# A decoder layer on one core: the steps of a round in another order on all engines

## What is computed

```python
x = _layernorm(x + _L0_attn_ref(x, ...))        # causal self attention, 16 heads of 16
#   local: softmax over the tokens before this one; latent: 4 heads over 50 averages of token pairs
#   gate = sigmoid(local @ gl_w + remote_h @ gr_w); mixed = gate*local + (1-gate)*remote_h; mixed @ out_w
x = _layernorm(x + _L0_xattn_ref(x, ctx, ctx))  # cross attention; queries and keys are normed in each head
x = _layernorm(x + _L0_ffn_ref(x, ...))         # top-1 of 8 experts, 200 tokens each; the rest pass through
```

## Time and profile before

| | us |
|---|---|
| median of 3 runs | 1654.99 |
| lowest and highest of them | 1653.84, 1660.99 |
| the profiled execution | 1657.47 |
| its span, first to last instruction | 1655.7 |

### The profile page before, as it was taken

How to read it: one execution, slowest core, us unless ns; L and a number is a source line. 1 busy time by engine, 2 the same in 40 slices (tenths; PEclk the granted TensorE clock), 3 DMA queues, 4 the chain that set the end, 5 groups by cost and what they waited for, 6 DMA issues and landing times.

```text
span 1655.7 us, 34010 instructions
## 1 busy us (share of the span) xinstructions
PE 1302.4 (79%) x11098; PEld 956.2 (58%) x11098; DVE 830.3 (50%) x2482; ACT 676.3 (41%) x1611; POOL 346.3 (21%) x485
## 2 busy tenths in 40 slices
PE   2577888788888878888888888887888888875886
PEld 2345666566565555555655566565555556554775
DVE  4255455555555555555555555555555555533332
ACT  0234444444444444444444444444444444533111
POOL 2122222221122222222222221122222222110111
PEclk8678777877777787888878787778777887755998
DMA  5233333323332232233333233332233233115452
GB/s 167 49 77 78 78 80 80 76 69 69 79 79 67 70 74 75 68 70 79 79 79 79 69 72 68 79 79 68 69 74 75 67 71 76 45 35 178 161 180 73
DMA packets 187013, 134.99 MB, mean 82 GB/s; under 512 B 95799, under 2 KB 182763, under 8 KB 186735
## 3 DMA queue, kind: packets, MB, share of 16 engines
q1 hardware_dynamic: 181778, 127.50, 30.7%
q0 software_dynamic: 3200, 6.61, 1.3%
q10 hardware_dynamic: 1984, 0.23, 0.1%
HBM read 91.06 MB, written 43.00 MB: 81 GB/s over the span
## 4 chain that ended last, share of the span: by engine, by line
PE 60%; issue 13%; DVE 9%; ACT 6%; POOL 6%; DMA 2%; ACTq 1%; SPq 1%; DVEq 0%; POOLq 0%
PE MI L809 12%; PE MI L810 11%; PE MI L1006 4%; PE MX L1122 3%; PE MX L975 3%; PE ST L993 3%; PE ST L870 3%; DVE negmax_x L1428 3%; DVE negmax_s L1421 3%; PE ST L875 3%; PE MX L837 2%; PE MI L955 2%; PE MX L843 2%; POOL mixed L711 2%; PE MI L919 2%
## 5 line engine op out<-in xcount | busy, mean ns | idle before, releaser
L1428 DVE TENSOR_REDUCE negmax_x<-MX 100x1 bf16<-100x361 f32 x512 | 258.0, 531 | 187.2 <-PE MX L975 185.1
L975 PE MATMUL MX<-stacked,Qst 96*128 96x361 f16 x512 | 180.5, 386 | 101.1 <-DVE negmax_x L1428 65.0
L1191 ACT ACTIVATE wide<-ST 128x800 f32<-128x800 f32 (+1 forms) x256 | 166.5, 665 | 144.9 <-PE ST L993 144.9
L975 PEld LDWEIGHTS MX<-stacked,Qst 96*128 96x128 f16 x512 | 52.6, 109 | 174.5 <-DVE negmax_x L1428 101.1
L993 PE MATMUL ST<-Qst,stacked 112*128 112x200 f16 x768 | 132.4, 301 | 0.2 <-ACT wide L1191 0.2
L700 POOL TENSOR_TENSOR QKhl<-QK,QKhl 128x900 f16<-128x900 f32 x32 | 60.5, 1892 | 182.8 <-ACT QKhl L1198 182.8
L993 PEld LDWEIGHTS ST<-Qst,stacked 112*128 112x128 f16 x768 | 82.2, 122 | 26.6 <-issue 11.2
L837 PE MATMUL MX<-mask_q,identb 100*128 100x400 bf16 (+1 forms) x128 | 43.0, 424 | 65.1 <-DVE negmax_s L1421 27.9
L1485 DVE TENSOR_TENSOR qn<-qc,rsq 128x200 f32<-128x200 f32 x32 | 11.8, 367 | 163.3 <-ACT rsq L1250 163.3
L1006 PE MATMUL MI<-wide,Vx 128*32 128x100 f32 (+1 forms) x3072 | 78.5, 261 | 1.3 <-ACT wide L1191 1.3
L734 POOL COPY x2w<-extra 100x2 f32 (+1 forms) x32 | 8.0, 248 | 340.8 <-issue 328.5
(11 more groups left out here) (259 smaller groups left out, 3050.5 us busy)
## 6 DMA issues: line engine op xcount, KB each, us to landing
stacked<-key_halves SPq DMA_DIRECT2D x96, 180.5 KB, 4.4
self_halves<-QKhl SPq DMA_DIRECT2D x32, 450.0 KB, 3.0
cT<-in_cT SPq DMA_DIRECT2D x32, 361.0 KB, 3.8
key_halves<-Khl SPq DMA_DIRECT2D x32, 361.0 KB
self_stack<-self_halves SPq DMA_DIRECT2D x64, 150.0 KB, 3.9
Qst<-query_halves SPq DMA_DIRECT2D x96, 100.0 KB, 2.6
early<-in_w SPq DMA_DIRECT2D x8, 1024.0 KB
self_stack<-self_halves SPq DMA_DIRECT2D x32, 225.0 KB, 3.8
```

The lines of the kernel that those rows point to most:

```text
L975: pe.matmul(MX[:, n % 2, 0:M], Qst[p][0:96, n * S:n * S + 128], Kst[p][0:96, n // 2 * M:(n // 2 + 1) * M], start=True, stop=True).then_inc ...
L1191: act.activation(cross_part(Px, u), ST[0:n, first:first + 2, 0:width], ACT.Exp).then_inc(st_exp, 1)
L1428: dve.tensor_reduce(negmax_x[:, n:n + 1], MX[0:S, n % 2, 0:M], X, ALU.max, negate=True).then_inc(max_read, 1)
```

## The change

The same steps run on each engine with the same waits, in another order. Besides the order within `body`, the list `MISC` is another one, so some steps take the other MI bank and wait for another step's copy. `MAXIMA` holds the same sequence, only broken into lines at another place.

```diff
--- before.py
+++ after.py
@@ -57,11 +57,11 @@
 OFFSET = {"T": -2, "Y": -1, "X": 0, "K": 1, "A": 2, "B": 1}
 
 
-MISC = ["A1", "A2", "K1", "B1", "T2", "K2", "B2", "T3", "K3", "T4", "B3", "K4", "B4", "T5", "A4",
-        "B5", "T6", "X1", "B6", "B7", "Y1", "K5", "Y2", "A6", "K6", "A7"]
-
...
+MISC = ["A1", "A2", "K1", "T2", "B1", "K2", "K3", "B2", "T3", "T4", "B3", "K4", "T5", "B4", "A4", "T6", "B5",
+        "B6", "X1", "B7", "Y1", "K5", "A6", "K6", "A7", "Y2"]
+
...
 
 SCORES = ["Y0", "Y1", "Y2", "Y3", "Y4", "Y5", "Y6", "Y7", "As0", "As1", "As2"]
 
@@ -600,17 +600,18 @@
             load_x(Seq(0))
 
             def body(it):
+                if it.n + 2 < B:
+                    load_n(Seq(it.n + 2, it.j))
                 if it.n + 3 < B:
                     load_x(Seq(it.n + 3, it.j))
-                if it.n + 2 < B:
-                    load_c(Seq(it.n + 2, it.j))
-                    load_n(Seq(it.n + 2, it.j))
                 if it.has("A"):
                     stack_self(it)
                 if it.has("K"):
                     stack_keys(it)
                 if it.has("B"):
                     stack_queries(it)
+                if it.n + 2 < B:
+                    load_c(Seq(it.n + 2, it.j))
 
             iterations(sp, body)
 
@@ -745,11 +746,10 @@
                 if a: pair_sums(A)
                 if b: gate_local(Bs, it)
                 if a: self_lo(it)
-                if b: gate_remote(Bs, it)
-                if b: mix(Bs)
+                if b: gate_remote(Bs, it); mix(Bs); query_low(it)
                 if t: keep_x2(T)
+                if b: x1_bias(Bs)
                 if t: scatter(T)
-                if b: query_low(it); x1_bias(Bs)
 
             iterations(pool, body)
 
@@ -1044,54 +1044,54 @@
 
             def body(it):
                 a, k, b, x, y, t = (it.has(stage) for stage in "AKBXYT")
+                if x: cross_maximum(it, 0)
                 if a: A1(it); A2(it)
                 if y: cross_scores(it, 0)
                 if k: K12(it, 0)
-                if x: cross_maximum(it, 0); cross_maximum(it, 1)
-                if b: B1(it)
+                if x: cross_maximum(it, 1)
                 if t: T2(it)
                 if x: cross_maximum(it, 2)
+                if b: B1(it)
                 if k: K12(it, 1)
-                if y: cross_scores(it, 1); cross_scores(it, 2)
+                if y: cross_scores(it, 1)
                 if x: cross_maximum(it, 3); cross_maximum(it, 4)
+                if k: K34(it, 0)
+                if x: cross_maximum(it, 5)
                 if b: B2(it)
-                if x: cross_maximum(it, 5)
                 if t: T3(it)
                 if x: cross_maximum(it, 6)
-                if y: cross_scores(it, 3)
-                if k: K34(it, 0)
+                if y: cross_scores(it, 2); cross_scores(it, 3)
                 if x: cross_maximum(it, 7); cross_maximum(it, 8)
                 if t: T4(it)
                 if x: cross_maximum(it, 9)
+                if y: cross_scores(it, 4)
                 if b: B3(it)
-                if y: cross_scores(it, 4)
                 if x: cross_maximum(it, 10)
                 if k: K34(it, 1)
-                if x: cross_maximum(it, 11)
+                if x: cross_maximum(it, 11); cross_maximum(it, 12)
+                if t: T5(it)
+                if y: cross_scores(it, 5)
+                if a: self_maxima(it, 0)
                 if b: B4(it)
-                if x: cross_maximum(it, 12)
-                if a: self_maxima(it, 0)
-                if y: cross_scores(it, 5)
-                if t: T5(it)
                 if a: self_maxima(it, 1)
-                if x: cross_maximum(it, 13); cross_maximum(it, 14)
+                if y: cross_scores(it, 6)
+                if x: cross_maximum(it, 13)
                 if a: A4(it)
-                if y: cross_scores(it, 6)
+                if t: T6(it)
                 if b: B5(it)
-                if x: cross_maximum(it, 15)
-                if t: T6(it)
+                if x: cross_maximum(it, 14); cross_maximum(it, 15)
+                if b: B6(it)
                 if y: cross_scores(it, 7)
                 if x: X1(it)
-                if b: B6(it)
-                if a: self_scores(it, 0); self_scores(it, 1)
+                if a: self_scores(it, 0)
                 if b: B7(it)
-                if a: self_scores(it, 2)
+                if a: self_scores(it, 1); self_scores(it, 2)
                 if y: Y1(it)
                 if k: K56(it, [0, 1])
-                if y: Y2(it)
                 if a: A6(it)
                 if k: K56(it, [2])
                 if a: A7(it)
+                if y: Y2(it)
 
             iterations(pe, body)
 
@@ -1275,35 +1275,35 @@
                 a, k, b, x, y, t = (it.has(stage) for stage in "AKBXYT")
                 if y: cross_exp(it, 0)
                 if k: K12(it, 0)
+                if t: copy_out("T2", it, OxT[:], halves)
                 if b: copy_out("B1", it, latT[:], lambda ps: ps[0:64, 0:S])
-                if t: copy_out("T2", it, OxT[:], halves)
                 if a: self_hi(it)
                 if k: K12(it, 1)
-                if y: cross_exp(it, 1); cross_exp(it, 2)
-                if t: rstd(it.of("T"), rs2, ln2, mv2, t_ln, t_rs)
+                if y: cross_exp(it, 1)
                 if k: K34(it, 0)
+                if y: cross_exp(it, 2)
                 if b: gate_exp(it)
-                if t: copy_out("T4", it, x2T[:], halves)
                 if y: cross_exp(it, 3)
+                if t: rstd(it.of("T"), rs2, ln2, mv2, t_ln, t_rs); copy_out("T4", it, x2T[:], halves)
+                if k: high_k(it, 0)
                 if b: copy_out("B3", it, mixT[:], halves)
-                if k: high_k(it, 0)
                 if y: cross_exp(it, 4)
                 if k: K34(it, 1)
+                if y: cross_exp(it, 5); cross_exp(it, 6)
                 if b: rstd(it.of("B"), rs1, ln1, mv1, b_ln, b_rs)
-                if y: cross_exp(it, 5)
+                if a: A4(it)
+                if b: copy_out("B5", it, x1T[:], halves)
+                if k: high_k(it, 1)
                 if t: router_exp(it)
-                if a: A4(it)
-                if k: high_k(it, 1)
-                if y: cross_exp(it, 6)
-                if b: copy_out("B5", it, x1T[:], halves)
+                if b: B6(it)
                 if y: cross_exp(it, 7)
                 if x: X1(it)
-                if b: B6(it)
-                if a: self_exp(it, 0); self_exp(it, 1)
+                if a: self_exp(it, 0)
                 if b: B7(it)
-                if a: self_exp(it, 2)
+                if a: self_exp(it, 1)
                 if b: high_q(it)
                 if y: copy_out("Y1", it, OxU[:], lambda ps: ps[:, 0:4 * S], (filled["Y2"], it.of("Y").done(back=1)))
+                if a: self_exp(it, 2)
                 if k: values(it, [0, 1])
                 if a: copy_out("A6", it, OsT[:], lambda ps: ps[:, 0:5 * S], (filled["A7"], it.of("A").done(back=1)))
                 if k: values(it, [2])
@@ -1575,32 +1575,31 @@
 
             def body(it):
                 a, k, b, x, y, t = (it.has(stage) for stage in "AKBXYT")
+                if x: cross_max(it, 0)
                 if a: A1(it); A2(it)
-                if x: cross_max(it, 0); cross_max(it, 1)
-                if x: cross_max(it, 2); cross_max(it, 3); cross_max(it, 4); cross_max(it, 5)
+                if x: cross_max(it, 1); cross_max(it, 2); cross_max(it, 3); cross_max(it, 4); cross_max(it, 5)
                 if b: B2(it)
                 if t: T3(it)
-                if b: gate_sum(it)
+                if b: gate_sum(it); gating(it)
                 if t: norm2(it)
-                if x: cross_max(it, 6); cross_max(it, 7)
-                if b: gating(it)
+                if x: cross_max(it, 6); cross_max(it, 7); cross_max(it, 8)
                 if k: key_norm(it, 0)
-                if x: cross_max(it, 8); cross_max(it, 9); cross_max(it, 10)
+                if x: cross_max(it, 9); cross_max(it, 10)
                 if k: key_low(it, 0)
                 if x: cross_max(it, 11); cross_max(it, 12)
+                if t: route_to(it)
+                if a: self_max(it, 0)
                 if b: B4(it)
-                if a: self_max(it, 0)
+                if a: self_max(it, 1)
                 if k: key_norm(it, 1)
-                if a: self_max(it, 1)
-                if t: route_to(it)
                 if b: norm1(it)
-                if x: cross_max(it, 13); cross_max(it, 14)
+                if x: cross_max(it, 13)
+                if t: place_in(it)
+                if x: cross_max(it, 14); cross_max(it, 15)
                 if k: key_low(it, 1)
-                if x: cross_max(it, 15)
-                if t: place_in(it)
                 if b: queries(it)
+                if a: A7(it)
                 if y: Y2(it)
-                if a: A7(it)
 
             iterations(dve, body)
 
```

4 lines of the change are left out of this document (2 added, 2 removed).

## The result

The changed kernel takes 1666.35 us (median of 7 runs, 1664.02 to 1671.62), the kernel before 1656.9 us (median of 7, 1653.84 to 1660.99): ratio 1.0061, 95% interval 1.0043 to 1.0079. It is slower by 0.6%, where 1.8% faster was forecast. The time lies in the range, next to the price of rival (c), but it is not rival (c) as I had it: the rounds came out neither at 43.2 nor at 44.7 us.

The account below looks back on a forecast made before the run. A chain from engine to engine up to B6, then TensorE's own work, bounds the round: 44.16 - 2.2 - 1.8 + 2.8 + 0.2 = 43.2 us. Over 30 rounds -30 us, giving 1625 us, range 1585 to 1668.

Parts of the forecast that it names:

- rival (c): Slower: X0 ahead of A1 waits for queries, then A1, A2 and K1 run at half clock; 44.7 us round, 1671 us; 20%.
- Gate and self maxima: From A1 through the gate: two waits become one and B4 moves back; self maxima at t 20.2 instead of 22.4, -2.2 us.
- B6: Self maxima to B6: this stretch takes 6.8 us instead of 8.6, -1.8 us; B6 starts at t 27.0 instead of 31.0.
- the gate's share: Gating directly behind its sum on VectorE: two waits of 3.7 us together become one of 3.0, a gain of 0.7 us.
- B6's place: On TensorE, B6 no longer stands behind T6, Y7 and the transpose X1, a gain of 1.0 us.
- B6 to the next A1: X0 ahead of A1 waits for the query stack; 15.9 to 16.0 us instead of 13.2, +2.8 us.
- The queue behind the keys: Query store waits behind key loads on the DMA engines; 0 to 1.0 us, taken as 1.0.
- Clock: Granted clock: half-clock cost at the head against a shorter half-clock stretch behind the gate, together +0.2 us a round.
- The +1.3 for the head: Clock falls at X0, so A1, A2 and K1 run at half clock; up to +1.7 us, taken as +1.3.
- The -1.1 against it: Half-clock stretch behind the gate is shorter than the 6.8 us assumed; 0 to -1.1 us, taken as -1.1.
- Rounds: Whole execution: a middle round's 1.0 us gain counted for 30 rounds, -30 us.
- SyncE: SyncE's context load moves to the round's end, behind the query loads; a margin remains, so no cost; otherwise 0.1 to 1 us.

Follow-up runs that it names:

- X0 back: Changed kernel with X0 returned to its old place, behind the first K12 on TensorE and its reduction behind A2 on VectorE; 1590.38 us, ratio 0.9602.
- the fillers at the gate: Changed kernel with X0 in its old place and SyncE's loads in the old order, plus 11 unread matmuls between X7 and X8; 1551.80 us, ratio 0.9375.
- short key loads: Changed kernel with the key-stack loads of the loop's rounds cut to 40 of 361 columns; 1650.74 us, ratio 0.9962.
- the kernel before with X0 ahead: Kernel before with only X0 moved ahead of A1 on TensorE and its reduction ahead of A1 on VectorE; 1721.41 us, ratio 1.0416.
- loads back: Changed kernel with SyncE's loads of x, context and rows in the order of the kernel before; 1664.61 us, ratio 1.0071.
- the kernel with both fillers: Changed kernel, X0 and SyncE's loads in old order, with 11 unread matmuls between X7 and X8 and 3 ahead of X13; 1519.14 us, ratio 0.9182.

## Why the prediction was wrong, point by point

**Gate and self maxima: -2.2 us, B6: -1.8 us.** Right in size together: with X0 back, the self maxima are 2.1 us earlier than before and B6 3.6 us (4.0 predicted), at t 20.30 and 27.54 for 20.2 and 27.0. But the working of the gate's share was wrong. I priced the gating's place at 0.7 us, the difference of the waits. Taken away, it costs 2.5 us, and given to the kernel before (together with ScalarE's part) it brings 1.3. The waits in sight differ by 1.1 us in the one pair (4.1 and 3.0) and by 0.6 in the other (3.7 and 3.1); the rest goes with the clock, whose half-clock time between t 12 and t 25 is on average 3.7 us longer in the one pair (9.4 and 5.8) and 2.0 in the other (7.2 and 5.2). That the clock makes up all of the rest is argued, not tested apart.

A reading was wrong too, that the self stack lands before t 19. In the kernel before its last load lands at t 19.8 on average, 3.8 us after its issue; that the DMA engines were through at t 18.7 was not yet the landing. The margin was half a microsecond, not one: in the changed kernel, where the stack lands at t 20.8, the self maxima wait for it in 4 of 23 middle rounds, and with the fillers at the gate in all.

**B6's place: 1.0 us.** Measured 1.1 us a round.

**B6 to the next A1: +2.8 us.** Measured +2.5 (15.76 for 13.25). The store came 8.74 us after B6 (8.8). The queue behind the keys, priced at the upper end of 0 to 1.0 us, was 0.4 us at the median of store to load (2.49 against 2.08), and 0.6 to 2.7 us in the rounds before 440 us. The store did wait for the keys, as the run with short key loads shows: the delay went with the keys' bytes. That agrees with the rule of the Trainium skill cited there ("DMA: Bandwidth & Descriptors", queues, rings and completion order), that on each DMA engine descriptors are consumed in ring order. TensorE's order was as the trace of before let expect: A1 starts 0.2 us after X0, never ahead of it.

**Clock: +0.2 us.** This is the term that failed in the middle rounds. The +1.3 for the head was near: X8 was 1.0 us later than with X0 back, and all that follows with it. But it was no sure thing. The clock fell at the head in 16 of 23 middle rounds, and in the kernel before with X0 ahead, where X0 waits 1.63 to 1.86 us, in none. The -1.1 against it wasn't there. From X8 to the self maxima it took 4.8 us, with and without X0 back, where 5.2 - 1.1 = 4.1 was my sum, and the clock was at half for 3.7 us of the 4.8 in both kernels. Even with the fillers at the gate and the clock at full there, the stretch takes 4.3 us, 1.2 of them the wait for the self stack. So the credit could not be had in full. By terms, the round is 16.52 (X8) + 4.80 + 7.11 (to B6) + 15.76 (to A1) = 44.19 us, where the sum has 16.3 + 4.1 + 6.8 + 16.0 = 43.2.

**Rounds: 30 times -1.0.** This step failed too, and it turned the sign from a gain of some 4 us (23 rounds of 0.16) to a loss. I multiplied a middle round by all rounds. In the first ones TensorE has less work between B6 and A1, so X0's wait is 4.3 and 4.9 us instead of 1.4, and the query store is held longer. By the ninth A1 15.9 us are lost, where my sum has 7 won (30 rounds less the 23 middle ones): 22.9 us. With X0 back they aren't lost (358.45 for 358.85), so it is X0's place that cost them. The middle rounds miss 23 x 0.84 = 19.3 us, and 1.9 us are lost behind them (12.2 us at the last A1 shown, 14.1 at the ends of the spans). Together that is the 44 us between the 30 us forecast as gain and the 14.1 us by which the profiled span grew.

**SyncE: no cost.** Right for this kernel (loads back: no difference), wrong as a statement about the load: the margin for the context was gone in early rounds, and it cost 1% as soon as X0's wait no longer covered it.

**The rivals.** (c) named the right mechanism, the wait of X0 together with the half clock at the head, and the point from which it decides: B6 later than t 28.2. B6 came at t 28.43. Its price for a middle round, 44.7 us, was too high by 0.5; its 1671 us came near only through the early rounds. I had kept it at 20% because I laid the head's cost and a gain behind the gate against each other as if they were sure to meet. And I never priced X0's move by itself. In its old place X0 had waited for its queries 3 times in the whole execution, so the move had nothing to win there, and the trace of before would have said so.

## What to carry to other kernels

Price a wait on TensorE with the granted clock of the dense work behind it, though the same length of wait brought the clock down in one kernel and not in the other, and count whether another wait follows close behind: here two waits of 3.1 and 1.1 us cost 2.5 us a round more than one of 3.0. Work in a queue must not stand at the head of others when it needs the end of a long chain: behind K12 X0 had almost no wait, ahead of A1 it cost over 4%. Before multiplying a round by their number, look at the filling rounds apart, where the work that hides a wait is not there yet.

## What the runs showed of the hardware

The clock fell behind much smaller waits than that of X0. In the round shown of the changed kernel waits of 0.43, 0.79 and 0.18 us with work between them were followed by 7 us at half clock. Between t 25 and t 38 it is at half for 6.1 us on average with the fillers at the gate alone; three unread matmuls (0.80 us) in the wait of 0.79 us made that 0.6 us. And 14 such matmuls in a round, which compute nothing, took the kernel from 1573.75 to 1519.14 us, 3.5%.

What the length of a wait doesn't tell is whether the clock falls. In the middle rounds of the changed kernel it fell behind 16 waits at X0, of 1.24 to 3.57 us, and not behind 7, of 1.08 to 1.35 us; in the kernel before with X0 ahead it fell behind none of 1.63 to 1.86 us. What makes the difference stays open.

Here a small store was held by loads issued well before it. With the store 4.8 us behind the last key load, store to first load is 2.08 us; 1.7 us behind (the changed kernel), 2.49 at the median; 0.73 us behind (the kernel with both fillers), 3.38; and 1.7 us behind loads of a ninth of the columns, 2.08 again.
